# Decoder layer on one Trainium2 core: norm statistics by halves, and the last FFN ticks spread around the third norm's turn

## What is computed

```
x = x + linear_attention(layernorm(x))        # r, k, v, g projections, decay, group norm, gate, Wo
x = x + cross_attention(layernorm(x), ctx)    # causal softmax over 16 heads, Wout
h = layernorm(x)
shared = silu(h @ sw_gate) * (h @ sw_up) @ sw_down
routed = sum over the best 2 of 8 experts of weight * (silu(h @ w_gate) * (h @ w_up)) @ w_down
x = x + routed + sigmoid(h @ shared_gate_w) * shared
```

## Time and profile before

| | |
|---|---|
| median of 3 runs (lowest, highest) | 692.47 us (691.09, 692.98) |
| the profiled execution: own time, span | 690.42 us, 688.7 us |
| mean granted clock | 0.973 |
| busy: PE, PEld, DVE, ACT, POOL | 92%, 74%, 56%, 39%, 49% |
| the chain that ended last: PE, DVE, POOL, issue, ACT | 53%, 19%, 14%, 7%, 5% |
| mean of one in the tick's chain: silu L761, product L1401, scale L599, high L751, low L589 | 374, 417, 736, 416, 766 ns |

### The profile page before, as it was taken

The page is one execution under the profiler, slowest core; times in us unless marked ns, Lnnn a source line. Parts: engine busy times, 40 slices in busy tenths (PEclk is TensorE's granted clock), DMA queues, the critical chain, the costliest instruction groups (busy, mean ns, idle before and its releaser), DMA issues.

```text
span 688.7 us, 16278 instructions
## 1 busy us (share of the span) xinstructions
PE 631.9 (92%) x6728; PEld 507.3 (74%) x6728; DVE 384.4 (56%) x780; ACT 269.7 (39%) x608; POOL 339.0 (49%) x474
## 2 busy tenths in 40 slices
PE   7887876799999999799999999799999999889997
PEld 6444455446979899545888889655879789779996
DVE  5997778688524554678533554779634244442120
ACT  4956123233234545242335545142334445143332
POOL 7673154223555656314455565313455555407666
PEclk9999989899999999999999999999999999979999
DMA  8911000020121111020120121011111111004220
GB/s 197 358 35 31 1 2 1 1 63 10 40 77 37 40 55 29 15 61 10 41 77 25 43 57 35 17 25 40 38 41 36 40 47 40 13 23 129 63 73 16
DMA packets 41540, 34.15 MB, mean 50 GB/s; under 512 B 9613, under 2 KB 40918, under 8 KB 41466
## 3 DMA queue, kind: packets, MB, share of 16 engines
q1 hardware_dynamic: 39562, 31.27, 16.3%
q10 hardware_dynamic: 1904, 1.84, 0.8%
HBM read 30.92 MB, written 2.17 MB: 48 GB/s over the span
## 4 chain that ended last, share of the span: by engine, by line
PE 53%; DVE 19%; POOL 14%; issue 7%; ACT 5%; DMA 1%; ACTq 0%; POOLq 0%; DVEq 0%
PE bank L984 6%; DVE A L1426 6%; PE bank L988 5%; PE bank L989 4%; PE bank L990 4%; PE bank L1156 4%; PE bank L1228 3%; POOL A L679 3%; POOL hT_last L687 3%; PE bank L1023 3%; DVE nm L1495 3%; POOL hb L599 3%; PE bank L1090 2%; PE bank L1025 2%; PE bank L1024 2%
## 5 line engine op out<-in xcount | busy, mean ns | idle before, releaser
L1401 DVE TENSOR_TENSOR hb<-hb,bank 128x256 f32<-128x256 f32 x102 | 42.5, 417 | 145.6 <-ACT hb L761 145.6
L589 POOL TENSOR_TENSOR hT<-hb,hT 128x256 fp32r<-128x256 f32 x102 | 78.2, 766 | 72.9 <-ACT hT L751 72.9
L599 POOL TENSOR_TENSOR hb<-hb,cwb 128x256 f32<-128x256 f32 x102 | 75.1, 736 | 78.1 <-DVE hb L1401 78.1
L751 ACT ACTIVATE hT<-hb 128x256 fp32r<-128x256 f32 x102 | 42.4, 416 | 131.3 <-POOL hb L599 131.3
L988 PE MATMUL bank<-xTf,wGh 128*128 128x256 f32 x272 | 83.5, 307 | 0.0
L1426 DVE TENSOR_TENSOR A<-bank,decay 128x512 f32<-128x512 f32 x128 | 77.4, 681 | 8.2 <-PE bank L1079 8.2
L989 PE MATMUL bank<-xTf,wGh 128*128 128x256 f32 x272 | 77.1, 284 | 0.0
L990 PE MATMUL bank<-xTf,wGl 128*128 128x256 f32 x272 | 77.0, 283 | 0.0
L989 PE MATMUL bank<-xTf,wUh 128*128 128x256 f32 x272 | 77.0, 283 | 0.0
L988 PE MATMUL bank<-xTf,wUh 128*128 128x256 f32 x272 | 76.9, 283 | 0.0
L990 PE MATMUL bank<-xTf,wUl 128*128 128x256 f32 x272 | 76.7, 282 | 0.0
(11 more groups left out here) (215 smaller groups left out, 1428.9 us busy)
## 6 DMA issues: line engine op xcount, KB each, us to landing
cwb<-cw_rows SPq DMA_DIRECT2D x54, 128.0 KB, 2.9
A<-cw_rows SPq DMA_DIRECT2D x18, 128.0 KB, 3.2
A<-in_x SPq DMA_DIRECT2D x4, 512.0 KB, 4.8
res<-in_x SPq DMA_DIRECT2D x4, 512.0 KB, 4.4
out_x<-res SPq DMA_DIRECT2D x8, 256.0 KB, 2.4
rawG<-in_L_ffn_w_gate SPq DMA_DIRECT2D x2, 704.0 KB, 7.0
rawU<-in_L_ffn_w_up SPq DMA_DIRECT2D x2, 704.0 KB, 7.2
cwb<-cw_rows SPq DMA_DIRECT2D x12, 112.0 KB, 2.8
```

The source lines that it names most:

```text
L589: pool.tensor_tensor(hT[:, c % 2, 1, :], hb[:, c % 2, :], hT[:, c % 2, 0, :].bitcast(F32), ALU.subtract).then_inc(h_lo, 1)
L599: pool.tensor_tensor(hb[:, c % 2, :], hb[:, c % 2, :], cwb[:, c % CWS, :], ALU.mult).then_inc(h_scaled, 1)
L751: act.activation(hT[:, c % 2, 0, :], hb[:, c % 2, :], ACT.Copy).then_inc(h_hi, 1)
L1401: tt(hb[:, c % 2, :], hb[:, c % 2, :], PS[5 + c % 2][:, HT:GT], ALU.mult).then_inc(gu_used, 1)
```

## The change

The statistics and aggregates of the second and third norm are issued per half: two sequences' statistics and aggregates stand behind that half's residual add, before the second half's add. The counts of the ticks change, `LAST` goes (all groups have the same counts), and two points are added: `r2` behind the turn, `r3` behind the first projection (behind the router in the last group). On TensorE the tick of `r1` is split: its gate-up stands before the turn, its down behind it. On DVE the second tick of `r0` moves ahead of `layer_apply`.

| ticks | n0 | n1 | n2 | n3 | n4 | n5 | x (12 points) | y0 | r0 | r1 | r2 | r3 |
|---|---|---|---|---|---|---|---|---|---|---|---|---|
| before, groups 1 and 2 | 1 | 2 | 3 | 2 | 2 | 2 | 20 | 1 | 3 | 1 | | |
| before, group 3 | 1 | 2 | 2 | 2 | 2 | 1 | 20 | 1 | 5 | 1 | | |
| after, all | 1 | 2 | 2 | 2 | 2 | 1 | 20 | 1 | 2 | 1 | 1 | 2 |

Ticks 31 and 32 then stand in `r0`, 33 in `r1`, 34 (down 32) in `r2`, 35 (down 33) and 36 (the residual) in `r3`.

```diff
-        POINTS = ["n0", "n1", "n2", "n3", "n4", "n5"] + [f"x{b}{p}" for b in range(GB) for p in "abc"] + ["y0", "r0", "r1"]
-        COUNT = dict(n0=1, n1=2, n2=3, n3=2, n4=2, n5=2, y0=1, r0=3, r1=1)
+        POINTS = ["n0", "n1", "n2", "n3", "n4", "n5"] + [f"x{b}{p}" for b in range(GB) for p in "abc"] + ["y0", "r0", "r1", "r2", "r3"]
+        COUNT = dict(n0=1, n1=2, n2=2, n3=2, n4=2, n5=1, y0=1, r0=2, r1=1, r2=1, r3=2)
-        LAST = dict(COUNT, n2=2, n5=1, r0=5)
...
@@ ScalarE, behind the two copies into xTf
                 for k in range(2):
                     act.activation(xTf[:, 0, k, :], PS[k][:, :], ACT.Copy).then_inc(xTf_hi, 1)
+                point(g, "r2")
+                point(g, "r3")
@@ TensorE
                 point(g, "r0")
+                if g:
+                    n = ticks_at(g, "r1")[0]
+                    assert n == FN - 1
+                    gate_up(g - 1, n)
                 turn_norm(2, g, tok2, 0)
-                point(g, "r1")
+                if g:
+                    down(g - 1, n - 2)
+                point(g, "r2")
                 if g + 1 < NG:
                     project(g + 1, 0)
+                    point(g, "r3")
                 pe.wait_ge(xTf_hi, g * 2 + 2)
...
                 last.then_inc(route_made, 1)
                 if g + 1 < NG:
                     project(g + 1, 1)
+                else:
+                    point(g, "r3")
                 pe.wait_ge(route_copied, g + 1)
@@ VectorE
+            def half_stats(s, src, q):
+                i = 0 if s == 0 else 1
+                for b in (2 * q, 2 * q + 1):
+                    nc.vector.bn_stats(st[:, i, b, :], src[:, b, :]).then_inc(ln_stats[s], 1)
+
+            def half_means(s, g, q):
+                i = 0 if s == 0 else 1
+                dve.wait_ge(ln_stats[s], g * 4 + 2 * q + 2)
+                for b in (2 * q, 2 * q + 1):
+                    nc.vector.bn_aggr(mv[:, i, b, :], st[:, i, b, :]).then_inc(ln_mean[s], 1)
...
                     tt(X[:, 2 * q:2 * q + 2, :], pair(PS[4 if q == 0 else 0]), X[:, 2 * q:2 * q + 2, :], ALU.add).then_inc(x1_ready, 1)
-                dve.wait_ge(x1_ready, g * 2 + 2)
-                layer_stats(1, g, X)
+                    dve.wait_ge(x1_ready, g * 2 + q + 1)
+                    half_stats(1, X, q)
+                    half_means(1, g, q)
...
                     tt(X[:, 2 * q:2 * q + 2, :], pair(PS[q]), X[:, 2 * q:2 * q + 2, :], ALU.add).then_inc(x2_ready, 1)
-                dve.wait_ge(x2_ready, g * 2 + 2)
-                layer_stats(2, g, X)
+                    dve.wait_ge(x2_ready, g * 2 + q + 1)
+                    half_stats(2, X, q)
+                    half_means(2, g, q)
                 if g:
                     ffn_tick(g - 1, ticks_at(g, "r0")[0])
                 if g + 1 < NG:
                     mixed_input(g + 1, 0)
+                if g:
+                    ffn_tick(g - 1, ticks_at(g, "r0")[1])
                 layer_apply(2, g, X, tok2)
-                if g:
-                    for n in ticks_at(g, "r0")[1:]:
-                        ffn_tick(g - 1, n)
                 point(g, "r1")
...
                     tt(xTf[:, 1, k, :], PS[k][:, :], xTf[:, 0, k, :].bitcast(F32), ALU.subtract).then_inc(xTf_lo, 1)
+                point(g, "r2")
+                point(g, "r3")
```

More of the change, by code:

```diff
@@ L379, in decoder_layer @@
                 COUNT[f"x{b}{p}"] = k
-        LAST = dict(COUNT, n2=2, n5=1, r0=5)
-        assert sum(COUNT.values()) == sum(LAST.values()) == TICKS
+        assert sum(COUNT.values()) == TICKS
         def ticks_at(g, point):
-            count = LAST if g == NG - 1 else COUNT
-            first = sum(count[p] for p in POINTS[:POINTS.index(point)])
-            return range(first, first + count[point])
+            first = sum(COUNT[p] for p in POINTS[:POINTS.index(point)])
+            return range(first, first + COUNT[point])
         SPLIT_AT_END = dict(act=("y0",) + tuple(f"x{b}b" for b in range(GB)), pool=("n2", "y0") + tuple(f"x{b}b" for b in range(GB)))
@@ L467, in _ @@
                 point(g, "y0")
-                point(g, "r0")
-                point(g, "r1")
+                for name in ("r0", "r1", "r2", "r3"):
+                    point(g, name)
                 sp.wait_ge(cwT_ready, g + 1)
```

## The result

The changed kernel takes 673.41 us (four runs, 672.39 to 673.99) against 692.72: a ratio of 0.9725, interval 0.9705 to 0.9744. It is 19 us faster, where 11.5 were forecast and the range ended at 674.5. In a later session it took 670.07, ratio 0.971 (0.9685 to 0.9734).

What follows compares the result with a forecast made beforehand. It took TensorE's idle time and slow clock as the bound. Halves -1.8, groups 1 and 2 -2.2 and group 3 -7.5 sum to -11.5: 690.42 to 678.9, plus 2.05 for the median, 681.0 us; range 674.5 to 687.5.

Steps and rivals of the forecast that it cites:

- part 1: Statistics and aggregates by halves in second and third norms: means come earlier; 1.8 us gained, bounds 0.9 and 3.9.
- part 2: Ticks leave n2 and n5 of groups 1 and 2, as group 3 already runs: gain 5.2 us in each.
- part 3: Tick 19 moves into `x1c` in groups 1 and 2, stalling TensorE: cost 3.5 us each, bounds 0 and 3.7.
- part 4: Third norm of groups 1 and 2: router 0.6 us later, with 4.26 us more work done; bounds 0 and 1.5.
- part 5: Group 3's third norm: routing 5.9 us earlier, then gate-ups at full clock; 7.5 us gained at the `cw` transposes.
- with the clock near 0.66 behind it: Sign: a new 1.7 us wait for the residual in groups 1 and 2, granted clock near 0.66 behind it.
- Rival B: No stall in `x1c`, if silu 18 came ahead of the exponentials: 7.0 us saved, 674 us; chance 0.09.
- the 15 that it had set as a sign of being wrong: Sign: forecast wrong if group 2's router follows the out projection by more than 15 us.
- The 1.8 us of `rstd`: Third norm, full lock-out by the mixed input: `rstd` takes 1.8 us and the turn comes 0.3 later.
- Rival A: Paced turn in groups 1 to 3 costs the clock: 5 us in all, 686 us; chance 0.24.
- C: Low parts come as late behind the turn: 3.7 us in three groups given back, 692.1 us; chance 0.09.
- D: Clock falls at the paced turn and stays low to the second projection: 21 us in three groups, 702 us; chance 0.06.

Runs made afterwards that it cites:

- kernel 7: Changed kernel with n5 at 2 ticks and r0 at 1, every tick between one place later: 668.8 us, ratio 0.969.
- kernel 6: The kernel before, unchanged, profiled once more: 688.6 us.
- kernel 8: Changed kernel with `layer_apply` of the third norm ahead of the second tick of `r0` on DVE: 673.5 us, ratio 0.974.
- kernel 10: The kernel before with 15 idle matmuls ahead of down 33 in the third norm of groups 1 and 2: 688.7 us, ratio 0.995.
- kernel 12: kernel 11 with 17 idle matmuls into free bank 4 in group 0's third norm: 667.0 us, ratio 0.966.
- kernel 1: The kernel before with statistics and aggregates of the second and third norm by halves, nothing else: 685.4 us, ratio 0.992.
- kernel 3: The kernel before with halves everywhere and the new tick places in group 3 alone: 676.6 us, ratio 0.979.
- kernel 11: kernel 7 with the next group's first mixed input moved behind `layer_apply` and product 33: 667.35 us, ratio 0.965.

## Why the prediction was wrong

The direction and the mechanisms held, the sizes of several terms did not. The result lies 7.6 us below the forecast (681.0) and 1 us below the range. From the stages of the two profiled executions, the forecast's terms against what they measured:

| term | forecast | measured |
|---|---|---|
| part 1, halves (both norms of group 0, second norms of the others) | -1.8 | -3.2 (0.4 + 0.8 + 3 x 0.68) |
| part 2, ticks out of n2 and n5, two groups | -10.4 | -10.1 (5.1 and 5.0, from the ticks alone) |
| part 3, stall in `x1c`, two groups | +7.0 | +3.4 |
| part 4, third norms of groups 1 and 2 | +1.2 | +0.3 |
| part 5, group 3 from its third norm to the end | -7.5 | -8.3 (6.2 + 2.1) |
| sum | -11.5 | -18.0 (of the unrounded terms) |

**The failed step is part 3:** "this is 75.57 - 0.4 - (72.68 - 1.0) = 3.5 us". It is mis-sized by 3.6 us for the two groups, over half of the 6.5 by which the sum is off. The stall, its place and its releaser were right, and kernel 7, where it is gone, shows that they were. Its price was read from one execution in which the clock had fallen behind it, and was carried over as if the fall belonged to the stall. The same stall without a fall costs 1.7. The idle row itself (1.71 in the earlier trace rows) had the answer; the 1.6 beyond it was a draw that came out otherwise in 17 of 20 cases. The sign "with the clock near 0.66 behind it" failed for the same reason: it was 1.00. Rival B, no stall, comes nearest in time (674) and was yet wrong: the stall is there three times.

**Part 1** took a wait's idle column (0.32) as its price. The same stretch, first gate-up behind the out projection to the turn, is 9.44 us before and 8.75 after, 0.69. The idle column counts from the modelled end of the last matmul (503.47), about 0.16 behind the point at which the next would have started at the usual distance; and the product behind the wait, like the first one of the next down, is followed 0.1 later than usual. These make up about 0.67 of the 0.69. "The second norm has ticks or idle products as cover" also failed in group 0 by 0.4: the turn there began behind the idle products, but was paced by `layer_apply` (1.41 against 1.04 us).

**Part 2** was right to 0.2 us in each group: group 3 of the kernel before already ran the new layout.

**Part 4** charged 0.9 us too much but placed the steps well: `layer_apply` 9.3 us behind the start of the out projection (forecast 439.6 - 430.3 = 9.3; measured 433.30 - 424.00), the turn's end 11.6 (forecast 11.8), router 17.1 (forecast 17.5), which is 13.5 behind the projection's end, within the 15 that it had set as a sign of being wrong. The added wait on DVE in `r3` was hidden: no wait of TensorE for it stands in the trace. TensorE is idle at the turn for 0.7 us and not 1.8, by the idle column, since it reached the turn at 9.3 and not at 9.0 and the pieces are short. The 1.8 us of `rstd` that the prediction estimated from the Trainium skill's rule leaves out that the mixed input had already run for 0.18 us when `rstd` started; the sum did not use it.

**Part 5**: router 14.6 us earlier in absolute time, 6.2 of it in this norm, forecast 5.7; 2.1 more came behind it, where the gate-ups ran at full clock. The `cw` transposes gained 8.4, forecast 7.5. Against the second profile of the kernel before (kernel 6) the two parts are 6.7 and 1.1, together 7.8, so half a microsecond of this term is the clock's draw.

**Rival A**, the paced turn costs the clock: in no profile of the new order did it fall there in groups 1 to 3 (7.3 us from turn to router in groups 1 and 2 of each that has it there; 8.06 and 8.08 in kernel 8, with its added wait). **C**, the idle time only moves: not so; in kernel 8, with one step swapped, some of it does (1.25, 1.24 and 0.66 us behind the turn). **D**, slower: no, the clock behind the turn stayed at 1.00.

The rest can be added up. The two profiled executions lie 16.7 us apart (690.42 and 673.73). The table's stages give 18.0 of gain and group 3's cross attention 1.6 more, since no clock fell there; group 0's cross attention takes 3.3 back (39.63 before, 42.88 after), and 0.3 are small differences elsewhere. The medians lie 19.3 apart because before's profiled execution was 2.3 us under its median and the changed kernel's 0.3 above. Which draws make up before's 2.3 is not shown.

## What to carry to other kernels

Price a stall by its idle time, and put half clock behind it as a separate term with a chance; look at whether the stretch that you copy from had granted clock 1.00. When a count shifts, look for the tick that carries something more than its neighbours (here the residual that frees a bank): one tick later its stall is gone (kernel 7). Where a wait can't be filled with work, matmuls into a free bank can pay if they end before it does: 3.3 us in kernel 10, no gain that the times can show in kernel 12.

## What the runs showed of the hardware

Half clock behind idle time of one length is not certain. Behind 1.7 us it came in 3 of 20 cases (1.6 us each), behind 3.15 us in two of four (groups 1 and 2 of kernels 1 and 3; 1.00 and 0.74 in the windows above of kernel 1), behind 3.7 us in all four of two executions of the kernel before. Both falls behind 3.15 us were in group 2, so with four cases a cause in the place is not excluded.

Group 0's cross attention, where no ticks fill TensorE's short waits, takes 39.6 to 40.1 us or 42.3 to 42.9 in executions of kernels that do not differ in it (9 and 5 of 14 profiles), granted clock 0.96 against 0.80 in the pair shown. A comparison of single runs of this kernel can be 3 us off for that alone.

POOL's `rstd` on four columns takes 1.05 us, and 1.48 when DVE's mixed input runs beside it; `ve`, ahead of it, takes 0.23 alone and 0.64 beside the mixed input. Moved apart, they take 1.05 and 0.23 (kernel 11). The Trainium skill, "SBUF — State Buffer", section "SBUF: two separate sides", which the prediction names, has such a pair shut each other out for the whole instruction of the one that starts first. By it `rstd` in the earlier trace rows would take 1.62 us, to the mixed input's end at 437.46 and 1.05 more (an estimate). The trace agrees in kind; with 1.48 it is 0.14 shorter.
